# The image rows of a deformable convolution contracted in fp32 straight from x, and its first image made inside the offset convolution

## The reference, cut to what matters

```
om = conv3x3(x, w_off) + b_off
py = om[:, :9]   + y + ky;   px = om[:, 9:18] + x_col + kx;   mask = sigmoid(om[:, 18:])
sampled[c, k, y, x] = mask * bilinear(x[c], py, px)          # 4 neighbours, zero outside
out = einsum('bckhw,ock->bohw', sampled, w) + b
out = relu(batchnorm(out)) + x
```

## Time and profile before

| | |
|---|---|
| three runs | 925.14, 930.49, 932.37 us; median 930.49 us |
| the profiled execution's own time | 933.15 us |
| its span, first to last instruction | 931.2 us |
| layer norm to attention, gate | 0 to 261 us |
| offset convolution | 261 to 318 us |
| image of pair 0, flag, first weights | 318 to 352 us |
| sampling loop | 352 to 906 us |
| batch norm, relu, residual | 906 to 931 us |

### The profile page before, as it was taken

How to read it: one execution, slowest core, us unless ns; L and a number is a source line. 1 busy time by engine, 2 the same in 40 slices (tenths; PEclk the granted TensorE clock), 3 DMA queues, 4 the chain that set the end, 5 groups by cost and what they waited for, 6 DMA issues and landing times.

```text
span 931.2 us, 31303 instructions
## 1 busy us (share of the span) xinstructions
PE 701.0 (75%) x11722; PEld 511.0 (55%) x11722; DVE 749.6 (80%) x1006; ACT 590.5 (63%) x1099; POOL 606.3 (65%) x391
## 2 busy tenths in 40 slices
PE   4886888887899778757776777785777767777753
PEld 2533555655335566646555656564656555565643
DVE  1447999998433448998989898997899879999985
ACT  1345667765212169777777787785878768777715
POOL 2004878883311207887888797887798779898970
PEclk9777999999899888898999998998899889999997
DMA  4000000000393345785775785855686585555402
GB/s 155 0 1 0 2 0 0 0 0 1 72 216 98 90 111 121 164 169 113 169 158 121 163 170 135 188 116 120 141 181 127 133 177 150 158 142 159 130 4 91
DMA packets 76059, 98.91 MB, mean 106 GB/s; under 512 B 53918, under 2 KB 57118, under 8 KB 75678
## 3 DMA queue, kind: packets, MB, share of 16 engines
q1 hardware_dynamic: 72928, 96.33, 43.9%
q10 hardware_dynamic: 3006, 0.84, 0.5%
HBM read 84.03 MB, written 6.42 MB: 97 GB/s over the span
## 4 chain that ended last, share of the span: by engine, by line
PE 36%; issue 21%; DVE 19%; SPq 10%; DMA 7%; ACT 4%; DVEq 1%; POOL 1%; ACTq 0%; POOLq 0%
PE PS L1166 35%; DVE region L819 6%; SPq L370 4%; DVE region L831 3%; DMA xr_scratch<-region 3%; SPq L362 2%; SPq L346 2%; DVE region L671 2%; DMA two<-xr_scratch 2%; DVE region L627 2%; DMA region<-px_scratch 2%; SPq L327 1%; ACT region L1061 1%; DVE region L631 1%; DVE region L646 1%
## 5 line engine op out<-in xcount | busy, mean ns | idle before, releaser
L1166 PE MATMUL PS<-region 64*64 64x144 f32 (+3 forms) x10112 | 468.0, 305 | 153.7 <-issue 109.1
L1166 PEld LDWEIGHTS PS<-region 64*64 64x64 f32 (+1 forms) x10112 | 362.4, 142 | 249.4 <-issue 220.0
L819 DVE TENSOR_TENSOR region<-PS,region 128x864 f32<-128x864 f32 x384 | 384.1, 1050 | 53.8 <-PE PS L1166 53.7
L528 POOL TENSOR_TENSOR region<-region 128x768 f32<-128x768 f32 x128 | 202.1, 1579 | 66.1 <-DVE region L819 66.1
L532 POOL TENSOR_TENSOR region<-region 128x864 f32<-128x864 f32 x128 | 223.8, 1748 | 27.4 <-DVE region L819 9.8
L1064 ACT ACTIVATE region<-region 128x1152 f32<-128x1152 f32 x128 | 149.2, 1165 | 57.3 <-PE PS L1166 53.8
L1061 ACT ACTIVATE region<-region,cst 128x1152 f32<-128x1152 f32 x128 | 159.3, 1245 | 22.9 <-DMA region<-px_scratch 21.8
L831 DVE TENSOR_REDUCE region<-region 128x32 f32<-128x960 f32 x128 | 146.3, 1143 | 1.5 <-POOL region L532 1.5
L441 POOL TENSOR_TENSOR region<-region,cst 128x1024 f32<-128x1024 f32 x32 | 61.5, 1922 | 52.2 <-ACT region L938 26.9
L1095 ACT ACTIVATE region<-x,cst (+2 forms) x288 | 86.7, 412 | 0.1
L671 DVE SCALAR_TENSOR_TENSOR region<-region,wr (+4 forms) x57 | 74.6, 1309 | 0.1
(11 more groups left out here) (128 smaller groups left out, 704.0 us busy)
## 6 DMA issues: line engine op xcount, KB each, us to landing
region<-px_scratch SPq DMA_DIRECT2D x256, 288.0 KB, 5.3
two<-xr_scratch SPq DMA_DIRECT2D x300, 16.0 KB, 4.2
xr_scratch<-region SPq DMA_DIRECT2D x8, 384.0 KB
out<-region SPq DMA_DIRECT2D x4, 512.0 KB, 3.0
x<-in_x SPq DMA_DIRECT2D x1, 1536.0 KB, 11.4
cst<-in_consts SPq DMA_DIRECT2D x1, 1234.5 KB, 7.9
region<-xp SPq DMA_DIRECT2D x8, 140.2 KB, 3.0
region<-xp SPq DMA_DIRECT2D x8, 140.1 KB, 3.0
```

What stands on the lines that cost most here:

```text
L528: pool.tensor_tensor(two_rows[:, :, :, 0:2 * THIRD - KEEP], two_rows[:, :, :, 0:2 * THIRD - KEEP], two_rows[:, :, :, KEEP:2 * THIRD], ALU. ...
L819: v.tensor_tensor(uu[:, 2 * u:2 * u + 2, :, THIRD * t:THIRD * (t + 1)], PS[:, 2 * t:2 * t + 2, 0:THIRD * C].rearrange("p h (a o) -> p h o ...
L1166: return nc.tensor.matmul(o, l, r, start=start, stop=stop)
```

## The change

The bf16 parts, their store, their loads and `px_done` go. `img` is made from `xp` where it lies: an image row is contracted over the 64 partitions of four images with weights that are zero for three of them (`wg`, 4 sets, built once on GpSimd). Pair 0's image, but for its last chunk (which the loop's first chunk makes, as before), is made between a chunk's offsets and its `to_samples`. For this `img` moves behind `xs` in SBUF, and `xs` of pairs 0 and 1 to the other region. `to_samples` has one pair of banks in place of two. SyncE loads the first px ahead of the flag. ScalarE makes pair 0's first vertical weights within the offset phase, VectorE finds the largest offset chunk by chunk, and SyncE's loops are written out.

```diff
+            pool.tensor_tensor(wg[:, :, :], mid(w_("w"), PAIRS), end(c_("bmod"), KK * C), ALU.mult).then_inc(wg_ready, 1)
...
+            def image_rows(g, y, bank, b):
+                for r in range(ROUNDS[b]):
+                    for h in range(2):
+                        part = slice(W * h, W * (h + 1))
+                        ins = mm(PS[part, bank, KK * C * r:KK * C * (r + 1)], xp3[part, y + 3 * b + r + 1, 1:1 + W], wg[part, g, :])
+                return ins
+
+            def first(n):
+                for b in range(3):
+                    q = 3 * n + b
+                    pe.wait_ge(fi_out, free(q))
+                    image_rows(0, RPC * n, 6 + q % 2, b).then_inc(fi_ready, 1)
...
             def to_samples(n, u):
                 pe.wait_ge(om_out, done(n, 2))
-                pe.wait_ge(py_out, free(n, 2))
-                pe.wait_ge(mk_out, free(n, 2))
+                pe.wait_ge(py_out, done(n - 1, 2))
+                pe.wait_ge(mk_out, done(n - 1, 2))
...
-            def slot_round(q, b, u, bank):
+            def slot_round(q, g, y, b, bank):
                 pe.wait_ge(row_out, free(q))
-                for r in range(3 * b, 3 * b + ROUNDS[b]):
-                    for h in range(2):
-                        at = KK * C * (r - 3 * b)
-                        ins = mm(PS[W * h:W * (h + 1), bank, at:at + KK * C], xrow[:, u, r, h, :], wsp[0:SPLITS * C, :])
-                ins.then_inc(slot_ready, 1)
+                image_rows(g, y, bank, b).then_inc(slot_ready, 1)
...
-                        if here:
-                            pe.wait_ge(xr_ready, s + 1)
```

On SyncE, behind the stores of px:

```diff
+            sp.wait_ge(om_ready, done(NCH - 1, 2))
+            for u in range(2):
+                sp.wait_ge(px_stored[u], 16 * B * NCH // 2)
+            for line in range(0, PXR, GR):
+                load_px(0, line, line)
             def load_ahead():
-                for line in range(0, PXR, GR):
-                    load_px(0, line, line)
-                sp.wait_ge(im_ready, done(NCH - 2))
-                load_rows(0, 0, NCH - 1, 1)
-                def chunk(g, c, rows, after):
...
+                for s in range(PAIRS * NCH - 1):
+                    g, c = (s + 1) // NCH, (s + 1) % NCH
+                    for line in range(0, RPC, GR):
+                        sp.wait_ge(wt_ready, done(s * SPC + line // GR))
+                        load_px(g, c * RPC + line, line)
```

On ScalarE, in place of the loop with L1044 and of pair 0's `image_chunk`:

```diff
+            def first_out(q, slot, b):
+                act.wait_ge(fi_ready, q + 1)
+                a.activation(img4[:, :, slot:slot + ROUNDS[b], :].rearrange("p k r o -> p r k o"),
+                             PS[:, 6 + q % 2, 0:KK * C * ROUNDS[b]].rearrange("p (r k o) -> p r k o", k=KK, o=C), ACT.Copy).then_inc(fi_out, 1)
...
+            for n in range(NCH):
+                act.wait_ge(om_out, done(n, 2))
+                store_px(act, n, n % 2, 1)
+                if n < NCH - 1:
+                    for b in range(3):
+                        first_out(3 * n + b, TOP + RPC * n + 3 * b, b)
+                samples_out(n)
+                if n == 2:
+                    act.wait_ge(py_out, done(0, 2))
+                    distance(0, 0, range(NR))
+                if n == 3:
+                    vertical_hat(0, 0)
```

More of the change, by code:

```diff
@@ L174, in build @@
         aw = cut(H * KK * NR)
+        img = cut(IR * KK * C)
         bns = aw[:, 0:6 * NCH]
@@ L345, in _ @@
                         a, b = (W + 2) * edges[j], (W + 2) * edges[j + 1] - kx
[L346 to L357, removed]
+                        sp.dma_start(xs_of(g)[32 * kx:32 * (kx + 1), a:b], xp[32 * g:32 * (g + 1), a + kx:b + kx]).then_inc(xs_in[j], 16)
+            for n in range(NCH):
+                sp.wait_ge(om_out, done(n, 2))
+                store_px(sp, n, n % 2, 0)
             def load_px(g, y, line):
@@ L364, in load_px, with pass_px @@
                                  ).then_inc(px_in[line // GR], 16)
-            def load_rows(count, g, c, u):
-                for slot, part in enumerate((0, 1, 2, 0, 1, 0)):
-                    for h in range(2):
[L370 to L373, removed]
-            def load_ahead():
-                for line in range(0, PXR, GR):
-                    load_px(0, line, line)
-                sp.wait_ge(im_ready, done(NCH - 2))
-                load_rows(0, 0, NCH - 1, 1)
-                def chunk(g, c, rows, after):
[L382 to L392, removed]
-                for c in range(NCH - 1):
-                    chunk(PAIRS - 1, c, False, (PAIRS - 1, c + 1))
-            def pass_px(p, g, band):
+            sp.wait_ge(om_ready, done(NCH - 1, 2))
[3 more added lines that the diff above has]
+                load_px(0, line, line)
+            def load_ahead():
+                for s in range(PAIRS * NCH - 1):
[3 more added lines that the diff above has]
+                        load_px(g, c * RPC + line, line)
+            def pass_px(p, g, band):
+                for line in range(0, PXR, GR):
+                    sp.wait_ge(px_in[line // GR], 32)
                 sp.wait_ge(wt_ready, p * STEPS + LAST)
@@ new lines, in _ @@
+            for n in range(NCH):
+                dve.wait_ge(om_ready, done(n, 2))
+                dve.wait_ge(tr_ready, free(n))
+                if n >= 2:
+                    dve.wait_ge(px_stored[n % 2], 16 * B * (n // 2))
+                for h in range(2):
+                    v.scalar_tensor_tensor(two[:, n % 2, h * CH:(h + 1) * CH], PS[:, 2 * h + n % 2, :],
+                                           bcol[:, :], c_("xg"), ALU.add, ALU.add).then_inc(om_out, 1)
+                if n >= 1:
+                    peak(n - 1)
@@ L810, in _ @@
             v.tensor_scalar(flag[:, :], small[0:1, 11:12], float(BR), None, ALU.is_gt).then_inc(flag_ready, 1)
-            with dve.Fori(2, NCH // 2) as step:
-                for u in range(2):
-                    stage(2 * step + u, u)
             def products(n, line, u):
```

201 lines of the change are left out of this document (62 added, 139 removed).

## The result

The changed kernel ran in 877.77 us, the median of 4 runs (876.57 to 878.17), and the kernel before in 927.82 us beside it on the same chip. The ratio is 0.9469, with a 95% interval of 0.9394 to 0.9543: 5.3% faster. The forecast was 883 us, the range 872 to 905. The profiled execution took 876.57 us, 1.9 us over its span of 874.7; the one before had a span of 931.2, so 56.5 us of span went. Executions over 1.5% above the fastest of their kernel are slow ones that no ratio uses, and the profiled one before (933.15 against 919.3) is such: some 5 of the 56.5 us belong to it. The medians lie 50 us apart.

The account below looks back on a forecast made before the run. VectorE was taken as the bound in pair 3, with waits for TensorE slowing pairs 0 to 2. The span 931.2 - 40 (loop) - 8.2 (start) - 0.4 (`selw` load) = 882.6 us gave forecast 883 us, range 872 to 905.

Parts of the forecast that it names:

- The loop's size: Sampling loop, pairs 0 to 2: without row transfers, steps run at pair 3's 3.98 us, gaining 40 us.
- DMA share near 0.47: Sign in the changed profile: the queue's busy share in the loop near 0.47 throughout, px loads landing in about 4.3 us.
- the rows cost more than their bytes: Loop's row transfers: 128-byte packets load the queue beyond their bytes; with bytes alone counting, gain near 12 us.
- SyncE no longer stands until they land: Loop: SyncE stops waiting for 12 row transfers a chunk before issuing px loads; part of the 40 us gain.
- the 12.7 points left over: Loop's queue share: 65.3% against 52.6% expected by bytes; the difference was read as the rows' extra cost.
- the long stalls stay: Rival, loop: px bursts, not rows, delay TensorE's instructions; gain 12 us, 911 us; chance 0.16 for wholly or half.
- Rounds in fp32: Loop's image rounds: fp32 round of 3 rows takes 0.74 us, hidden by VectorE, costing 0 us.
- rounds as the bound: Rival, loop: fp32 rounds exceeding TensorE's 1.39 us spare per step push VectorE; up to 971 us, chance 0.03.
- corners that don't overlap: Rival, fp32 image work: array corners run serially; offset phase grows 26 us, loop pays 5; 902 us, chance 0.10.
- Offset phase: Offset convolution: the image chunk moved inside adds 1.96 us a period, making 8.6 us; phase 12.3 us longer.
- T: End of the last chunk's offsets in the offset convolution, predicted at 324.9 us.
- Behind T: From the last offsets' end to the loop's first product: 18.6 us, product at 343.5 us, gain 8.2 us.

Follow-up runs that it names:

- e1: Kernel before without the loop's row transfers except the first two batches, whose rows are contracted again: 890.06 us, ratio 0.959.
- e5: Changed kernel plus twelve 16 KB transfers a chunk in 128-byte rows, ahead of the px loads, into an unread buffer: 913.04 us, ratio 0.9861.
- e6: Changed kernel plus twelve 16 KB transfers a chunk in 1 KB rows, ahead of the px loads, into an unread buffer: 909.68 us, ratio 0.9805.
- e8: Changed kernel plus twelve small transfers a chunk in 128-byte rows, spread three behind each two px loads: 884.23 us, ratio 0.9545.
- e2: Kernel before with all row transfers, but TensorE waits for the rows itself and SyncE goes on to the px loads: 919.4 us, ratio 0.9874.
- e7: Changed kernel, no transfer added; in pairs 0 to 2 a chunk's px loads wait for its third step and go out together: 925.55 us.
- e9: Changed kernel with every fp32 round of pairs 0 to 2 made twice into the same banks: 879.92 us, ratio 0.9453.
- e10: Changed kernel with pair 0's image, except its first chunk, made behind the offset convolution and the flag's matmul: 873.7 us, ratio 0.9388.
- e11: Changed kernel with the first eight px loads issued in the branch behind the flag: 881.58 us, ratio 0.9488.
- e12: Kernel before with its twelve row transfers a chunk spread, four behind each of the first three pairs of px loads: 914.27 us, ratio 0.984.

## Why the prediction was right, and where its steps were not

*Direction and sum.* Right: 877.77 against 883. The sum gave 884.6 us of own time, and the profile has 876.57: 8.0 us less. Of these 3.1 are the loop (43.1 in place of 40) and 4.8 the start (13.4 in place of 8.6). Some 5 us of both belong to the one execution that the sum started from: the medians differ by 50 us, and with 11 to 12 at the start (below) the loop's part is 38 to 39, so the 40 was no underestimate.

*The loop's size.* Right. "Pairs 0 to 2 then load as pair 3 does": steps of 3.95 us (3.98 with all stalls, the very rate of pair 3 before), VectorE's wait under 5 us (1.3), no long piece of "issue". The 1.8 us that I left for the first steps were not needed. The transfers and their wait alone are worth 36 us (e1). "DMA share near 0.47" was wrong, at 0.58: pair 3's window holds fewer loads.

*The loop's cause.* Here a step failed: "the rows cost more than their bytes", by packets, and "SyncE no longer stands until they land". Measured one by one, the packets cost 3 us (e5 against e6) or 6.5 with their issues (e8), and the wait 7 to 12 (e2). What cost more is the order of issue: twelve issues ahead of eight large loads hold SyncE 6 us or more, and the loads go out as one burst (e5, e6: 32 to 35 us), and a burst alone does the same (e7: 34 to 47 us). So the size of the loop's gain came out by luck in part: removing the transfers removed the bursts too, whichever of the two had cost the time. The share of the queue, from which I read the cost of small packets, does not predict the time: 72.3% gave 884 us (e8), 56.5% gave 912 to 925 (e7). Nor are the 12.7 points left over the packets' alone. The queue was busy 3.7 us for each MB in pair 3 before and in the changed kernel, 4.6 in the kernel before and 4.5 in e8 with small packets spread, but 4.3 also in e7, which has not one small packet more: a burst alone does most of that. The Trainium skill's rule on 512 bytes ("DMA: Bandwidth & Descriptors", Specifications) is not refuted by this: 128-byte rows do take more of the queue (67.0 against 65.1% for fewer bytes). It was the wrong rule to read the stalls by.

*The rival "the long stalls stay".* Its mechanism was right, px loads in bursts that make TensorE's instructions late, and its outcome wrong, since the bursts themselves came from the rows. I had set the two against each other as if one excluded the other. The rows that would have told are of SyncE's timeline in the kernel before, which I had not read so; in pair 0 and in pair 3:

```profile
405.75 5.44 SPq L362 DMA_DIRECT2D region<-px_scratch  x8
411.46 5.68 SPq L370 DMA_DIRECT2D two<-xr_scratch  x12
...
777.62 61.65 SPq L362 DMA_DIRECT2D region<-px_scratch  x32
```

Eight px loads go out in 5.44 us in pair 0, and in pair 3 32 of them take 61.65 us, 1.9 each. That it is the fetching of instructions that the bursts delay is shown by the instruction packets beside the stalls of e5, e6 and e7. Why such a packet starts late while px packets move, no run shows.

*Rounds in fp32.* 0.74 us predicted, some 0.7 measured, hidden as predicted; even twice as many are (e9). The rival of rounds as the bound is out. The rival of corners that don't overlap is out too: 69 ns an instruction in the image chunks, a wait included, where no overlap meant 122. The Trainium skill ("FP8 and Floating Point Precision", TensorE Precision Notes) has fp32 as four passes; the 69 ns hold them, as I had taken it.

*Offset phase.* The mechanism was right, a term too small: 9.05 us in place of 8.6 a period. 0.26 us of this is the image chunk, and not its rate: TensorE's timeline has 24 of its weight loads in 1.42 us, 59 ns each, and then a wait of 0.16 us for ScalarE to empty the first round's bank (1.1 us in 7 such waits from 257 to 330 us), where the prediction had "no wait". 0.20 is the convolution and `to_samples` beside it (6.83 us; in e10, without the image, they take 6.64). Over six periods that is 2.7 us. ScalarE's nine distances did not cost the 1.2 us. T on the old start is 326.5, against 324.9. (The bound of 26 us for corners that don't overlap counted seven chunks; six lie ahead of T, some 24 us.)

*Behind T.* Too long by 2.2 us: the first product at T + 16.4, not T + 18.6. The last stores were issued by T + 5.4, not T + 6.5, and the px loads went out 1.3 us behind them, at T + 6.8, not at T + 9.2; the row of the `xs` loads (2.7 us) was too dear for stores of `px`. From there on the terms held: 5.2 us to the first hat (4.9 predicted), two hats, and 2.0 us to the first product. The flag (330.82) was not last, as I had it; but it would have been in the way, and loading px ahead of it is worth 3.8 us (e11).

*The start ahead of the change's place.* The offset convolution begins at 257.09, 4.7 us before the 261.76 of the trace of before. The `selw` load, a term of 0.4 us in the sum that no row gave, explains 0.2: the first matmul starts at 10.12 in place of 10.29. In the profiles of e1, e2 and e12, which have before's start, it begins at 258.07 to 258.33, so some 3.5 us belong to that one execution. Their first products lie at 349.56 to 350.66. The change's own gain at the start is then 11 to 12 us of the 13.4.

*Work moved to where it seemed free.* I counted the image inside the offset phase against its removal behind it and found a gain. Both hold against before, but e10 shows the better place: TensorE waits for px behind the flag anyway.

## What to carry to other kernels

Before blaming a queue's share or its packets, lay its issue times beside the waits: many small issues ahead of large loads make one burst of them, and the burst is what stalls others; spreading the issues won 29 us here (e5 to e8) at a higher share. Long pieces of one wait cost and many short ones do not, since a step's slack takes in each piece up to its own size. Work moved off a path belongs where its engine waits, not into a phase where that engine is the bound.

## What was not expected

- Loads in a burst cost 34 to 47 us with not one byte more and next to no wait for them (e7), by TensorE's "issue" in pieces up to 5.1 us. The granted clock went with the stalls: 0.99 in the changed kernel from 343 to 766 us, 0.92 in e7, 0.98 in e8. The stall comes first: each of the 16 stretches at half clock in e7's loop (345 to 766 us, 71.7 us in sum) begins during or behind a stop of TensorE of over 1.2 us. What the half clock adds to the cost was not measured apart.
- Doubling the rounds made the "issue" wait of TensorE smaller, 40.0 us in place of 60.4 from 345 to 766. Part of "issue" is thus time that the engine has over, not a loss.
- VectorE's product takes 1,064 ns in the changed kernel and 1,048 in e7; over 384 products that is 6 us. It stays open why; it does not go by the waits, since e8 and e1, which wait little, have 1,047 and 1,045.
- What lies ahead of the offset convolution differs by up to 3.7 us between executions of kernels that are the same there (258.07 to 261.76), more than some terms of the prediction.
